# Depthwise products of a windowed-attention layer in 64x32 tiles by patch half, the 1x1 products in 64x64 quadrants, border rows corrected by GpSimd

## The reference, cut to what matters

```
x: (4, 64, 128, 128) fp32
xn  = group_norm(x, 32 groups)                     # 2 channels a group, over H and W
qkv = w_qkv (192x64) . xn + b_qkv                  # 1x1 convolution, 64 -> 192 channels
qkv = depthwise_3x3(qkv, w_dw, zero padding) + b_dw
# windows of 8x8 pixels, 4 heads of 16 channels; q, k, v: (window, head, 16, 64 pixels)
attn = softmax(q k^T * temperature)                # 16x16 for a head: a sum over the 64 pixels
out  = attn v * gelu(w_mlp (64x64) . v + b_mlp)    # gate over the pixels of a window
y    = x + w_proj (64x64) . out + b_proj
```

## Time and profile before

| | |
|---|---|
| median of three runs | 678.43 us (677.24 to 682.87) |
| profiled execution, span of the core | 680.0 us |
| TensorE busy | 625.8 us (92%), 15044 MATMUL and 15044 LDWEIGHTS |
| DVE, ACT, GpSimd busy | 511.6 (75%), 482.8 (71%), 0.3 us |
| mean granted clock of TensorE | 0.973 of full speed |

### The profile page before, as it was taken

One profiled execution on the slowest core, in us unless ns is written; L12 is line 12 of the kernel. 1 busy time (PEld: TensorE's weight loads), 2 busy tenths in 40 slices (PEclk: granted clock), 3 DMA queues, 4 the chain that ended last, 5 costly groups with the idle time before them and its releaser, 6 DMA issues.

```text
span 680.0 us, 32438 instructions
## 1 busy us (share of the span) xinstructions
PE 625.8 (92%) x15044; PEld 549.1 (81%) x15044; DVE 511.6 (75%) x790; ACT 482.8 (71%) x631; POOL 0.3 (0%) x5
## 2 busy tenths in 40 slices
PE   3788799999999999999999999999999999999954
PEld 2687698888989898888989898888989798888843
DVE  4872688887888888786878676786868676876684
ACT  3652678787877778786877778786877778786722
POOL 0000000000000000000000000000000000000000
PEclk9997899999999999999999999999999999999975
DMA  9872115335171714132050504132150504112022
GB/s 363 263 217 72 33 50 166 110 86 208 33 232 49 234 59 149 66 102 93 8 191 5 195 4 142 60 94 106 29 173 4 198 3 152 44 50 80 4 82 44
DMA packets 29240, 72.28 MB, mean 106 GB/s; under 512 B 9801, under 2 KB 16329, under 8 KB 24233
## 3 DMA queue, kind: packets, MB, share of 16 engines
q1 hardware_dynamic: 28674, 68.57, 31.0%
q10 hardware_dynamic: 432, 1.65, 0.7%
HBM read 53.44 MB, written 16.78 MB: 103 GB/s over the span
## 4 chain that ended last, share of the span: by engine, by line
PE 87%; ACT 5%; DVE 3%; issue 2%; DMA 1%; ACTq 0%; DVEq 0%
PE unit_ps L709 28%; PE unit_ps L674 26%; PE rest_ps L796 10%; PE rest_ps L787 6%; PE rest_ps L763 6%; PE rest_ps L747 6%; PE rest_ps L773 4%; ACT z L326 2%; DMA patches<-in_hot 1%; ACT dw L326 1%; PE rest_ps L643 1%; PE rest_ps L674 1%; PE unit_ps L636 0%; DVE scores L511 0%; DVE scores L536 0%
## 5 line engine op out<-in xcount | busy, mean ns | idle before, releaser
L326 ACT ACTIVATE z<-unit_ps 100x768 f32<-100x768 f32 x244 | 184.9, 808 | 60.1 <-PE unit_ps L674 60.1
L674 PE MATMUL unit_ps<-consts,patches 64*100 64x192 f32 x1984 | 195.0, 336 | 8.6 <-ACT z L326 6.6
L709 PE MATMUL unit_ps<-z,dw 103*64 103x64 f32 (+2 forms) x6144 | 194.3, 224 | 3.0 <-issue 1.7
L709 PEld LDWEIGHTS unit_ps<-z,dw 103*64 103x64 f32 (+2 forms) x6144 | 185.5, 139 | 10.7 <-issue 8.6
L674 PEld LDWEIGHTS unit_ps<-consts,patches 64*100 64x100 f32 x1984 | 153.6, 164 | 25.8 <-ACT z L326 11.2
L326 ACT ACTIVATE qkv<-unit_ps 128x1024 f32<-128x1024 f32 x78 | 79.1, 1014 | 31.5 <-PE unit_ps L709 31.4
L511 DVE TENSOR_TENSOR scores<-rest_ps,consts 128x512 f32<-128x512 f32 x64 | 44.1, 689 | 51.6 <-PE rest_ps L747 51.6
L503 DVE TENSOR_TENSOR gate<-rest_ps,gate 128x512 f32<-128x512 f32 x64 | 44.1, 689 | 47.5 <-PE rest_ps L787 44.6
L796 PE MATMUL rest_ps<-gate,consts 128*128 128x256 f32 x256 | 75.1, 417 | 1.1 <-DVE gate L503 1.0
L347 ACT ACTIVATE v_t<-rest_ps 128x512 f32<-128x512 f32 x64 | 38.2, 597 | 40.5 <-PE rest_ps L773 38.9
L341 ACT ACTIVATE scores<-scores 128x512 f32<-128x512 f32 x64 | 40.4, 631 | 33.2 <-DVE scores L518 31.6
(11 more groups left out here) (55 smaller groups left out, 530.5 us busy)
## 6 DMA issues: line engine op xcount, KB each, us to landing
staged<-in_x SPq DMA_DIRECT2D x17, 1024.0 KB, 4.9
out_y<-staged SPq DMA_DIRECT2D x15, 1024.0 KB, 5.4
T<-in_x SPq DMA_DIRECT2D x12, 1152.0 KB, 6.7
seen<-in_x SPq DMA_DIRECT2D x32, 256.0 KB, 2.9
qkv<-in_x SPq DMA_DIRECT2D x6, 1024.0 KB, 13.9
T<-in_x SPq DMA_DIRECT2D x3, 1088.0 KB, 6.7
staged<-in_x SPq DMA_DIRECT2D x2, 512.0 KB, 22.9
out_y<-staged SPq DMA_DIRECT2D x4, 256.0 KB, 3.0
```

Of the source, the lines that this page charges most:

```text
L326: return nc.scalar.activation(to, of, ACT.Copy)
L674: last = nc.tensor.matmul(to[0:NPATCH, t, b * QKV:(b + 1) * QKV], patches[image, b, g], w1[image], start=True, stop=True)
L709: last = nc.tensor.matmul(to[h * HW:(h + 1) * HW, m // 8, m % 8 * NW:(m % 8 + 1) * NW], dw[0:used, c, :], z[0:used, c, :], start=True, sto ...
```

## The change

The patch of 10x10 pixels is laid out in 104 rows: patch rows 0 to 5, four bias lines, patch rows 6 to 9. Half `r` = 0 of the partitions takes rows 0 to 63 (patch rows 0 to 5 and the lines), half `r` = 1 rows 40 to 103 (patch rows 4 to 9 with the lines before them), 64 rows each; each half yields 4 of the 8 output rows, 32 pixels. A mix call becomes two, of 64x64 (8 calls in a unit). A dw call becomes two of 64 rows x 32 output pixels (64 calls in a unit); for every second head of Q and K the two pixel halves trade places in the output, and scores sum over pixels, so Q and K stay matched. `dw` has 32 columns instead of 64 and is built in 4 steps instead of 8; its table `hot` has its own SBUF tensor. The copies to `z` add a column of 0/1 (`lines`) to set the bias lines, so they cover 128 partitions and are bias activations on ACT and `tensor_scalar` on DVE. The DMAs into rows of `z` are gone; instead GpSimd subtracts b_qkv from the 10 pixels of the patch row that lies outside the image, in the four edge bands (chunks 0, 7, 8, 15), 6 instructions each over 32 partitions, once mix copies of four groups are done; the first dw unit of such a chunk waits for them. `normalise` becomes two instructions (60 and 40 of 100 pixels).

```diff
@@ 
-NPATCH = PATCH * PATCH
-EDGES = 9
-K = NPATCH + EDGES
+SHARED = 4 * PATCH
+UPPER = 6 * PATCH
+LINES = 4
+PITCH = UPPER + LINES + SHARED
+OUTS = HW // 2
+RIM = 32
-BUILDS = HW // (PX * TILES)
+BUILDS = OUTS // (PX * TILES)
@@ 
+def rim_pieces(q):
+    lo, hi = 4 * q, 4 * q + 4
+    if q == 0:
+        return [(1, lo, lo + 1), (0, lo + 1, hi)]
+    if q == 3:
+        return [(0, lo, hi - 1), (2, hi - 1, hi)]
+    return [(0, lo, hi)]
@@ def evacuate_mix(engine, add, n, g):
-            copy(z[0:NPATCH, :, 4 * g:4 * g + 4].rearrange("p c (b t) -> p c b t", t=2),
-                 work[buffer(unit)][0:NPATCH, :, 0:2 * QKV].rearrange("p t (b c) -> p c b t", b=2)
-                 ).then_inc(free[buffer(unit)], 1)
+            add(z[:, :, 4 * g:4 * g + 4].rearrange("p c (b t) -> p c b t", t=2),
+                work[buffer(unit)][:, :, 0:2 * QKV].rearrange("p t (b c) -> p c b t", b=2),
+                line_of(g)).then_inc(free[buffer(unit)], 1)
@@ sync
-                if 0 < n % BANDS < 5:
-                    for p in range(4):
-                        top_rows(n // BANDS, 4 * (n % BANDS - 1) + p)
@@ gpsimd
+            def outside(n, q):
+                for g in range(4 * q, 4 * q + 4):
+                    if n:
+                        wait_free(pool, ("mix", n, g))
+                    else:
+                        pool.wait_ge(first_free[g % 4], q + 1)
+                b = 0 if band_of(n) == 0 else 1
+                rows = slice(0, RIM) if b == 0 else slice(P - RIM, P)
+                for kind, lo, hi in rim_pieces(q):
+                    at = z[rows].rearrange("p c (g b t) -> p c g b t", b=2, t=2)[:, :, lo:hi, b]
+                    less = rim[rows, kind].unsqueeze(2).unsqueeze(3).to_broadcast([RIM, QKV, hi - lo, 2])
+                    nc.gpsimd.tensor_tensor(at, at, less, ALU.subtract).then_inc(rimmed, 1)
+            for n in range(CHUNKS):
+                if at_edge(n):
+                    for q in range(4):
+                        outside(n, q)
@@ def normalise(n, b, at=0, size=COLS):
+                for lo, hi, to in ((0, 6, 0), (6, PATCH, UPPER + LINES)):
...
@@ def mix_group(to, g):
-                        last = nc.tensor.matmul(
-                            to[0:NPATCH, t, b * QKV:(b + 1) * QKV],
-                            patches[image, b, g], w1[image],
-                            start=True, stop=True)
+                        for r in range(2):
+                            px = slice(r * SHARED, r * SHARED + HW)
+                            last = nc.tensor.matmul(to[r * HW:(r + 1) * HW, t, b * QKV:(b + 1) * QKV],
+                                                    patches[image, b, g, px], w1[image], start=True, stop=True)
@@ def depthwise(n, v):
-                for m in range(SPLIT):
-                    for h in range(2):
-                        c = kind * C + h * HALF + at + m
-                        last = nc.tensor.matmul(to[h * HW:(h + 1) * HW, m // 8, m % 8 * NW:(m % 8 + 1) * NW],
-                                                dw[0:used, c, :], z[0:used, c, :], start=True, stop=True)
+                if v == 0 and at_edge(n):
+                    pe.wait_ge(rimmed, RIM_PIECES * sum(at_edge(m) for m in range(n + 1)))
+                for m, e, r, h in product(range(SPLIT // 2), range(2), range(2), range(2)):
+                    c = kind * C + h * HALF + e * SPLIT + at // 2 + m
+                    rows = slice(r * HW, (r + 1) * HW)
+                    side = r if kind == 2 else r ^ e
+                    out_rows = slice(h * HW + side * OUTS, h * HW + (side + 1) * OUTS)
+                    last = nc.tensor.matmul(to[out_rows, e, m * NW:(m + 1) * NW], dw[rows, c], z[rows, c],
+                                            start=True, stop=True)
```

More of the change, by code:

```diff
@@ L1 @@
 from contextlib import ExitStack
+from itertools import product
 import numpy as np
@@ L100, in looks_until, with build @@
     return min(i // BATCHES * sum(LOOKS) + sum(LOOKS[:i % BATCHES]), STATS)
-def build(nc, x, taps, hot, edges, weights, out):
+def build(nc, x, taps, hot, rims, weights, out):
     with ExitStack() as ctx:
@@ L326, in copy, with add @@
                 return nc.scalar.activation(to, of, ACT.Copy)
+            def add(to, of, line):
+                return nc.scalar.activation(to, of, ACT.Identity, bias=line)
             def evacuate_build(m):
@@ L366, in _ @@
             exp_table(0)
+            act.wait_ge(consts_in, 16)
             for g in range(0, COLS, 2):
-                evacuate_first(act, copy, g)
+                evacuate_first(act, add, g)
             for v in range(0, 6, 2):
@@ L382, in _ @@
                         for g in range(8 * a + 2, 8 * a + 6):
-                            evacuate_mix(act, copy, n, g)
+                            evacuate_mix(act, add, n, g)
                 if a == 2:
@@ L408, in _ @@
                 if more and a < 2:
-                    evacuate_mix(act, copy, n, 8 * a + 6)
-                    evacuate_mix(act, copy, n, 8 * a + 7)
+                    evacuate_mix(act, add, n, 8 * a + 6)
+                    evacuate_mix(act, add, n, 8 * a + 7)
         @block.vector
@@ L417, in copy, with add @@
                 return nc.vector.tensor_copy(to, of)
+            def add(to, of, line):
+                return nc.vector.tensor_scalar(to, of, line, None, ALU.add)
             def link(ins):
@@ L484, in normalise @@
                 pair = n // BANDS
[L485 to L489, removed]
+                for lo, hi, to in ((0, 6, 0), (6, PATCH, UPPER + LINES)):
+                    rows = T[:, b * WS + lo:b * WS + hi, at * WS:]
+                    line = rows.ap[1][0]
+                    windows = bass.AP(rows.tensor, rows.offset,
+                                      [rows.ap[0], [WS, size], [line, hi - lo], [1, PATCH]])
+                    held = patches[:, b, at:at + size, to:to + (hi - lo) * PATCH]
+                    last = nc.vector.tensor_scalar(held.rearrange("p w (r c) -> p w r c", c=PATCH), windows,
+                                                   norm[:, pair, 0:1], norm[:, pair, 1:2], ALU.subtract, ALU.mult)
                 if b == 1:
@@ L578, in _ @@
             for g in range(1, COLS, 2):
-                evacuate_first(dve, copy, g)
+                evacuate_first(dve, add, g)
             pads(1)
@@ L837, in _, with _row @@
             project(STEPS - 1)
-_ORDER = ("x", "taps", "hot", "edges", "weights")
+_ORDER = ("x", "taps", "hot", "rims", "weights")
+def _row(y, x):
+    return y * PATCH + x + (LINES if y >= 6 else 0)
 def _hot():
[L845 to L857, removed]
@@ L860, in _edges @@
[L860 to L868, removed]
+    hot = np.zeros((TAP_ROWS, OUTS, 2, HW), np.float32)
+    for r in range(2):
+        line = UPPER - r * SHARED
+        for y in range(WS // 2):
+            for x in range(WS):
+                at = hot[:, y * WS + x, r]
+                for tap in range(TAPS):
+                    dy, dx = divmod(tap, 3)
+                    at[tap, _row(4 * r + y + dy, x + dx) - r * SHARED] = 1
+                    left, right = x == 0 and dx == 0, x == WS - 1 and dx == 2
+                    at[TAPS + tap, line:line + 3] = (1, -left, -right)
+                at[2 * TAPS, line] = 1
@@ new lines, in _hot, with _rims, _lines @@
+    return hot.reshape(TAP_ROWS, BUILDS, TILES, PX, P).transpose(2, 0, 1, 3, 4).reshape(P, BUILDS * PX * P)
+def _rims(b_qkv):
+    rims = np.zeros((P, 3, QKV), b_qkv.dtype)
+    for at in (0, P - PATCH):
+        rims[at:at + PATCH] = b_qkv
+        rims[at, 1] = 0
+        rims[at + PATCH - 1, 2] = 0
+    return rims.reshape(P, 3 * QKV)
+def _lines():
+    lines = np.zeros((P, 3), np.float32)
+    for at in (UPPER, HW + UPPER - SHARED):
+        lines[at] = 1
+        lines[at + 1, 1] = 1
+        lines[at + 2, 2] = 1
+    return lines
@@ L906 @@
         "hot": _hot(),
[L907 removed]
+        "rims": _rims(b_qkv),
         "weights": np.concatenate([
```

74 lines of the change are left out of this document (36 added, 38 removed).

## The result

The changed kernel takes 855.86 us (median of four, 853.62 to 858.76) against 678.13 before; the ratio is 1.261, interval 1.256 to 1.266. The forecast was 815 us, its range 715 to 885.

The account below looks back on a forecast made before the run. TensorE was taken to bound the kernel, its instruction fetch just escaped at 3.8 us per line. Terms of +97, +8, -18, +45, +5 and -1 gave +136 on 680.0, so 815 us, range 715 to 885.

Parts of the forecast that it names:

- line: 256 TensorE instructions, fetched as one 16 KB packet; claimed to cost 3.5 us each, with only one fetched ahead.
- array sets the time: Rival: the array, not instruction fetch, sets the time of TensorE's units; 650 us; chance 0.09.
- Further lines ahead: Rival: TensorE's instructions are fetched more than one line ahead, so bursts average out; 715 us; chance 0.06.
- The tiles do nothing: Rival: in dw units 64x32 tiles overlap by four only and lines come fast; 665 to 680 us; chance 0.03.
- Two of the signs named: Expected in the new profile: granted clock low in the dw half's stretches; ACT and DVE busy times unchanged within 3%.
- dw half: Half of a period with dw units: 25.5 us against 19.0 by lines of 3.5 us; fifteen chunks, +97.
- mix half, gain and losses: Half with mix units: -1.2 us for unchanged array shape, +3 for late lines and clock; fifteen times, -18 and +45.
- border work: GpSimd's subtraction in four edge bands: 0 to 6 us a band exposed, +5 taken in all.
- up to the first score, with the first dw units: Six first dw units take 22.5 us against 14.6, +8; smaller `hot` frees DMA time, -1.
- the two ends: In the dw half, about half a line before the first and after the last line entered, unhindered: 2.2 us.
- The rule of 25 ns: Skill's rule that TensorE starts are never under about 25 ns apart: dw unit 3.2 us, whole about 805 us.
- The array alone, 650 us: The rival array sets the time, chance 0.09: four dw units save 0.93 us each, but little comes out.

Follow-up runs that it names:

- a_dw_wide: Changed kernel with 64x32 tiles kept but half the dw calls, each streaming 128 columns, so 128 instructions a unit: 679.4 us, ratio 1.002.
- a_no_rims: Changed kernel without GpSimd's border subtraction and TensorE's wait for it: 849.8 us, ratio 1.254.
- a_bare: Changed kernel with plain copies to `z`, without GpSimd's border subtraction, and with one row of `T` loaded per chunk: 819.2 us, ratio 1.207.
- b_mix_split: Kernel before the change with only each mix call cut in two, on 64x64 quadrants: 661.4 us, ratio 0.975.
- a_copy: Changed kernel with plain copies to `z` on ACT and DVE, bias lines left out: unclear, 848 to 873 us in four runs.
- a_t_short: Changed kernel with one row of `T` loaded per chunk instead of 18: 842.1 us, ratio 1.232.

## Why the prediction was right, and where its sizes were off

**The bound and the line.** The step that carried the forecast held. A dw unit of 256 instructions costs a line; the end-to-start anatomy read off two stray pauses came back in the 81 pauses of the changed kernel: TensorE resumes 1.38 us after a packet's end (median, and 1.2 to 1.6 in 79 of them), the next packet starts 1.16 us after that, and these packets last 1.00. That is 3.54 us. None of the 182 packets is nearer than 3.28 us to the one before. The rival *array sets the time* fails by a_dw_wide, read the other way: the array would have gained, but only with the old number of instructions. *Further lines ahead* fails with the pauses themselves, 256 instructions apart. *The tiles do nothing* fails by the 0.89 us of a K unit against 1.6 of a V unit in a_dw_wide. What the Trainium skill has (Advanced Engine Details and Errata, ISA Cache), lines of 256 instructions and only two of them, agrees with the 182 packets of 16 KB and with the pauses; its 128 KB for TensorE does not show.

Two of the signs named came out otherwise. The granted clock was not simply low in the dw halves: 0.93 of full speed on the mean, and within 1% of full speed in five of fifteen. And busy times did not stay within 3%: ACT's rose by 4.3% (482.8 to 503.4 us) by its dearer copies to `z`, DVE's by 3.7% (511.6 to 530.5), in part by what it loses beside GpSimd; both are told below.

**The sum, term by term.** Starting at the first score product, 66.7 us before and 82.4 after, the fifteen periods took 577.0 and 735.7 us.

| term | forecast, us | measured, us |
|---|---|---|
| dw half | 15 x 6.5 = 97 | 15 x 9.2 = 138 (28.3 for 19.1, mean of 15) |
| mix half, gain and losses | 15 x (3 - 1.2) = 27 | 15 x 1.4 = 21 |
| border work | 5 | in the rows of the dw half and of the first score; 6 by a_no_rims |
| up to the first score, with the first dw units | 8 - 1 = 7 | 15.7 |
| last steps | 0 | 0.4 |

So the mechanism was right and the size of the dw half was off by 41 us. That this equals the whole difference of 41 is luck: the first units were forecast 9 us too low, and the mix half and the border's own term 11 too high, which nearly cancel.

Of the 2.7 us that were missing per half, border work took 0.7: the halves that prepare chunks 7, 8 and 15 are 30.2, 33.0 and 30.0 us, the other twelve 27.6. In those twelve the packets are 3.67 us apart on the mean, not 3.5, which gives 6.66 x 0.17 = 1.1 us. The remaining 0.9 us falls to the two ends, set at 2.2 us in all. The clock has a part in both: the five halves within 1% of full clock, none with border work, average 27.2 us. How much of the ends is the clock's and how much was guessed too short was not separated, since the clock can't be set in an experiment. a_bare, without border work, still has 28.3 us a half, with more of them at a lower clock.

**Mix half.** The gain for the unchanged shape of the array was taken as 1.2 us. In b_mix_split it is 1.6 in undisturbed halves (17.3 for 18.9) and 1.2 on the mean of fifteen. The changed kernel keeps less: ACT's copy with a bias takes 0.90 us on the mean instead of 0.81, which I had passed over with "as wide as now". Its fastest mix half is 18.0 us against 17.3. That ACT holds it is read from the profiles: TensorE's weight loads waited 33 us for ACT, and with plain copies the fastest mix half is 17.4 us, in a_copy and in a_bare. The total time of a_copy was unclear. The longer mix halves go with a lower clock: the five at full clock average 19.0 us, the ten others 21.6. a_t_short gave back 14 us in all; in its profile the first score comes 7.0 us earlier and the mix halves are 0.9 us shorter, while the dw halves are 0.5 us longer.

**First units.** 52.97 to 79.86 is 26.9 us for 14.6, where 22.5 were forecast. The line with the packet behind `T`'s load took 7.3 us, 3.8 more than the others (3.5 to 3.7 each) where 3 were taken, and the two ends 3.3 and 2.2 us where 2 were taken for both. GpSimd kept TensorE waiting for 3.8 us more before them.

**GpSimd.** A round of 1536 elements takes 2.9 us, 1.4 times the 2.1 that DVE would need, within the bounds. The cover of about 2 us ahead of the dw unit was too thin, as the row of chunk 15 shows. Yet removing it all gave back 6 us, not the 13.3 that TensorE waited. In the profile of a_no_rims the places themselves gave back 16 us: the first score comes 7.4 us earlier, the dw halves before chunks 8 and 15 are 5.6 and 3.3 us shorter, that before chunk 7 is not. The other halves were longer, the mix halves above all (21.2 for 20.8 us on the mean, at 0.79 to 0.87 of the clock in the three worst). Whether that follows from the edit or is the spread of executions is open.

**The rule of 25 ns.** A number near mine, 805, came from the Trainium skill's issue gap (TensorE: Matmul & The Clock Gate). The trace does not bear it out across tiles: 176 MATMULs start in 2.59 us, at most 14.7 ns from one to the next on the mean, and then a pause follows.

**The array alone, 650 us.** With the instructions back at 128 a unit, the changed kernel reaches 679, not 650. Its undisturbed halves are about as short as this rival had them, 18.0 and 18.0 us. It left out the waits for GpSimd (dw halves of 21.1, 22.3 and 20.0 us before chunks 7, 8 and 15, and dw units that begin at 53.1 us instead of 47.9) and the clock, with three mix halves of 19.9 to 21.2 us at 0.91 or 0.92.

## What to carry to other kernels

Count TensorE's instructions as a resource beside its busy time: with one line of 256 ahead and 3.5 to 3.7 us for each, it sustained no more than about 70 instructions per us here, and an fp32 matmul call here is four of them. A split of a product into smaller tiles pays where instructions are sparse (the mix products, -2.5% alone) and loses where they are dense already (the dw products stood at 3.8 us a line). Before halving a call, look for the longest mid-unit pause labelled "issue" beside the instruction queue's packets: two such pauses held the whole forecast.

## What the runs showed of the hardware that was not expected

- DVE's `scores - neg_max`, with both operands in SBUF, took 2.06 us in the row above and 1.16 to 2.61 us in all six executions that fell beside GpSimd's `tensor_tensor`, against 0.69 us otherwise; over the run its 64 instructions cost 52.4 us instead of 44.3. Without GpSimd's work (a_no_rims) it was 44.3 again. The reduction just ahead of it in the timeline kept its 0.69 us.
- Cutting the moving columns from 64 to 32 leaves the rate of MATMULs at 29.5 ns on two 128x64 tiles; each loads the weights of 64 columns, which is the likely reason.
- An ACT copy from PSUM over 128x768 takes 0.81 us as a plain copy and 0.90 us with a bias column.
- 64x32 tiles overlap more than four deep: 64 MATMULs of 128 columns take 1.16 us on eight tiles, and start within 0.89 us where four tiles need 1.6.
